# One Mamba block between two feed-forward blocks: GpSimd's running sum of squares moved behind the other work of its pass in one pass of four

## The reference

```python
x = x + 0.5 * ffn(layernorm(x))      # weights by index from a table of 16 values, inner width 688
x = x + mamba2(layernorm(x))
x = x + 0.5 * ffn(layernorm(x))
```

```python
gate, hbc, dt = split(h @ in_proj_w)                # 4096 | 4096 + 2*128 | 64
x, B, C = split(silu(conv4(hbc) + conv_b))          # causal convolution over 4 tokens
y = chunked_scan(x, B, C, softplus(dt + dt_bias), A) + D * x
hidden = y * silu(gate)
var = mean(hidden * hidden, axis=-1)
out = (hidden * rsqrt(var + eps) * norm_w) @ out_proj_w
```

## Time and profile before

| | us |
|---|---|
| median of three executions | 1468.12 (1466.66 to 1471.08) |
| profiled execution, its own time | 1469.74 |
| span of its profile | 1468.0 |
| TensorE busy | 1336.6 |
| VectorE busy | 1190.8 |
| ScalarE busy | 1007.1 |
| GpSimd busy | 823.1 |

### The profile page before, as it was taken

The page is one execution under the profiler, slowest core; times in us unless marked ns, Lnnn a source line. Parts: engine busy times, 40 slices in busy tenths (PEclk is TensorE's granted clock), DMA queues, the critical chain, the costliest instruction groups (busy, mean ns, idle before and its releaser), DMA issues. The chain is left out here.

```text
span 1468.0 us, 27111 instructions
## 1 busy us (share of the span) xinstructions
PE 1336.6 (91%) x8896; PEld 1137.1 (77%) x8896; DVE 1190.8 (81%) x2643; ACT 1007.1 (69%) x2067; POOL 823.1 (56%) x896
## 2 busy tenths in 40 slices
PE   5889887767999999999999999999999999986998
PEld 4778776556888888888888888888888888864887
DVE  5753443576999999999999999999999999986433
ACT  1114433667889988888988898888899888861332
POOL 1004211004678787877878787797787878681000
PEclk9999987978999999999999999999999999995999
DMA  6221000223454554454564645644435544324000
GB/s 128 66 87 36 15 15 0 65 65 76 121 111 98 118 125 114 119 112 98 119 125 115 118 101 114 116 123 121 113 101 109 129 113 117 96 73 186 15 14 29
DMA packets 102085, 136.43 MB, mean 93 GB/s; under 512 B 27744, under 2 KB 49856, under 8 KB 101824
## 3 DMA queue, kind: packets, MB, share of 16 engines
q1 hardware_dynamic: 99840, 132.67, 37.6%
q10 hardware_dynamic: 2112, 2.10, 0.4%
HBM read 124.76 MB, written 9.96 MB: 92 GB/s over the span
## 5 line engine op out<-in xcount | busy, mean ns | idle before, releaser
L845 ACT ACTIVATE M<-cum_row,cum_table 128x128 f32<-128x128 f32 x1024 | 312.2, 390 | 0.0
L1240 DVE SCALAR_TENSOR_TENSOR xs<-psum,conv_w_sb,xs 128x509 f32<-128x509 f32 (+2 forms) x384 | 284.2, 740 | 0.4
L985 POOL TENSOR_TENSOR hid_lo<-hid,hid_hi 128x512 fp32r<-128x512 f32 x128 | 191.2, 1494 | 65.4 <-PE psum L40 59.6
L1028 POOL TENSOR_TENSOR hid<-hid,sg 128x512 f32<-128x512 f32 x128 | 165.7, 1295 | 89.5 <-DVE hid L1308 89.4
L1017 POOL TENSOR_TENSOR squares<-squares,sq 128x512 f32<-128x512 f32 x124 | 160.2, 1292 | 75.2 <-ACT sq L822 75.2
L1267 DVE TENSOR_TENSOR M<-M,CB 128x1024 f32<-128x1024 f32 x128 | 182.9, 1429 | 0.0
L1623 PE MATMUL psum<-M,xdt 128*64 128x128 f32 x2048 | 140.1, 279 | 20.8 <-DVE psum L1299 20.8
L827 ACT ACTIVATE sg<-psum 128x512 f32<-128x512 f32 x128 | 75.2, 587 | 102.2 <-PE psum L40 94.6
L1623 PEld LDWEIGHTS psum<-M,xdt 128*64 128x64 f32 x2048 | 109.9, 136 | 43.2 <-DVE M L1267 25.0
L1600 PE MATMUL psum<-xend,B_tok 128*128 128x128 f32 x1024 | 140.3, 281 | 2.1 <-DVE carry L1291 1.9
L859 ACT ACTIVATE xs<-psum,conv_b_sb,conv_w_sb 128x512 f32<-128x512 f32 x128 | 98.7, 771 | 52.7 <-PE psum L40 52.7
(11 more groups left out here) (210 smaller groups left out, 3432.5 us busy)
## 6 DMA issues: line engine op xcount, KB each, us to landing
cum_row<-cum_scratch SPq DMA_DIRECT2D x256, 256.0 KB, 4.6
e_row<-e_scratch SPq DMA_DIRECT2D x256, 128.0 KB, 3.5
xw_raw<-L_attn_in_proj_w_dram SPq DMA_DIRECT2D x32, 128.0 KB, 5.1
wo_raw<-L_attn_out_proj_w_dram SPq DMA_DIRECT2D x32, 128.0 KB, 4.6
gw_raw<-L_attn_in_proj_w_dram SPq DMA_DIRECT2D x16, 256.0 KB, 5.8
x_res<-_attn_hidden_states_dram ACTq DMA_DIRECT2D x4, 512.0 KB, 9.3
x_scratch<-x_res SPq DMA_DIRECT2D x4, 512.0 KB, 2.6
x_res<-x_scratch SPq DMA_DIRECT2D x1, 2048.0 KB, 7.6
```

The source lines that it names most:

```text
L845: last = nc.scalar.activation(M[:, v % 3, h, c * CH:(c + 1) * CH], cum_row[:, v % 2, h, c * CH:(c + 1) * CH], ACT.Relu, bias=scalar_of(CUM ...
L985: nc.gpsimd.tensor_tensor(hid_lo[:], hid[:, v % 2, :], hid_hi[:, v % 2, :].bitcast(F32), ALU.subtract).then_inc(hid_lo_done, 1)
L1028: nc.gpsimd.tensor_tensor(hid[:, v % 2, :], hid[:, v % 2, :], sg[:, v % 8, :], ALU.mult).then_inc(hid_done, 1)
L1240: nc.vector.scalar_tensor_tensor(xs[:, v % 7, shift:], psum[:, X_BANK + v % 2, 0:TT - shift], tap_of(v, step), xs[:, v % 7, shift:], ALU.m ...
```

## The change

In passes with s % 4 = 1 GpSimd's `add_squares(s)` moves from the head of the pass to behind the gate, the split of hid and, in slot 1, the split of the last output weights. In the code it stands ahead of the other weight splits of the slot table (x weights of slot 5, gate weights of slot 9, output weights of slot 13). In all other passes nothing changes.

```diff
             for s in range(-8, ALL):
-                if alive(s):
+                after_silu = s % GP == 1
+                if alive(s) and not after_silu:
                     add_squares(s)
                 if s == 1:
                     fold_dt(1)
...
                 g, u = divmod(s, SLOTS)
                 if g > 0 and u == 1:
                     split_wo(g * GP + GP - 1)
+                if alive(s) and after_silu:
+                    add_squares(s)
                 if s < 0 or g == GROUPS - 1:
                     continue
                 if u in X_SLOTS:
```

## The result

| | us |
|---|---|
| changed kernel, median of 5 executions | 1480.57 (1480.31 to 1483.36) |
| kernel before, median of 5 executions | 1468.12 (1466.21 to 1471.08) |
| ratio | 1.0086, 95% interval 1.0069 to 1.0103 |
| span of the changed kernel's profile | 1478.6 |

The change makes the kernel 12.4 us slower. The forecast was 1478.6.

A forecast was written before the change was run, and what follows sets the result against it. TensorE was taken to bound the group loop except at named waits. 8.8 us (gate weights) plus 1.7 us (slow clock), all else 0, made 10.5 us on a 1468.1 us median: 1478.6 us, range 1471.5 to 1487 us.

The forecast's parts named there:

- The main term: Slot 9: the moved sum delays the gate weights' low half and so TensorE, 7 x 1.26 = 8.8 us.
- The head of the pass: Where the sum leaves: the gate gains 0.6 us, the low half nothing as it waits for TensorE; worth 0.
- The other signs: Sums wait few us for ScalarE; L1299 scaling wait stays near 17.5 us; no new TensorE waits on ScalarE/VectorE over 5 us.
- The clock term: After the longer gate-weight waits in the loop: one 3.4 us stretch at 1.2 GHz, 1.7 us; bounds 0 to 12.
- Slot 1: Sum behind the output weights makes the square 3.9 us late, VectorE 0.3 us, seven times; taken as 0, bounds 0 to 2.1.
- Rival 2: ScalarE becomes late: later squares in slots 1, 5 and 9 reach TensorE, 4.2 us on top, 1482.8 us; chance 0.12.
- slots 5 and 9: The square starts about 2.5 us later there, hidden in ScalarE's idle time ahead of L827; cost 0.
- rival 4: Faster: the seven gate-weight waits vanish, 5.6 us, and slot 13's gate avoids the product, 3.6 us; 1458.9 us, chance 0.06.
- Beside VectorE: The moved sum runs beside the convolution taps, not the product L1267; cost 0, otherwise 0.73 us in some of 32 passes.
- Rival 3: The sum is hidden: gate weights are ready as before since the low half starts sooner; 1468.1 us, chance 0.09.
- The smaller form of rival 3: Slot 9: 0.34 us gained of each 1.26 us, leaving 6.4 us in all.

The follow-up runs named there:

- experiment 1: Changed kernel, but with the sum of slot 9 back at the head of the pass: 1472.3 us, ratio 1.0025 to the kernel before.
- experiment 2: Kernel before, with the sum moved in slot 9 alone: 1478.8 us, ratio 1.0071.
- experiment 3: Changed kernel, with the sum behind all weight splits of its pass: 1479.4 us, ratio 1.0075 to the kernel before.
- experiment 11: Kernel before, with slot 9's gate weights split first, low halves held behind VectorE's product (s % 4 = 0), slot 9's sum behind the hid split: 1447.7 us.
- experiment 7: Changed kernel, with the low half of the gate weights computed twice in slot 9: 1498.3 us, ratio 1.0201 to the kernel before.
- experiment 5: Kernel before, with the sum moved in slot 1 alone: 1472.2 us, measured once.
- experiment 6: Kernel before, with the sum moved in passes 121 and 125 alone: 1470.3 us, measured once.
- experiment 9: Kernel before, with GpSimd's low half of hid (in slot 0 also the gate) held behind VectorE's product where s % 4 = 0: 1457.8 us, ratio 0.9929.

## Why the prediction was right

*The main term* was right in place, cause and size. It gave 7 x 1.26 = 8.8 us in front of the gate weights; slot 9 measured 8.6, the wait of TensorE 14.2 us where 14.4 were forecast. Experiments 1 and 2 show it from both sides. The head of the pass was worth nothing. In slot 9 that is for the reason given: the low half waits for TensorE. In slot 13 it is not: there the low half starts 1.8 us sooner in the pass, and no slot from 13 to 15 is shorter for it. The sum is harmless to the gate weights once they are split ahead of it, which experiments 3 and 11 show in two ways. The other signs came as listed: sums waited 7.2 us in total for ScalarE, TensorE's wait for the scaling stayed at 17.5 us, and its only new waits on VectorE are 1.7 us in slot 4.

*The clock term*, one slow stretch at 1.7 us, came out as one stretch at 1.6. That it was one and not none or four was luck; experiment 2 had one in seven as well. That such a wait can bring a slow stretch is shown by experiment 7, six of seven, and the cost of one stretch is 1.5 to 1.6 us. Which of seven equal waits is followed by one, no run tells. The full clock of the earlier trace rows begins with the eleventh slice, at 367 us, and not with the ninth; nothing in the sum hangs on it.

*Slot 1* was traced to the right chain and then costed at 0 inside bounds of 0 and 2.1 us. It measured 1.5 us. The step that failed is the one that said "the next named wait of TensorE is a full pass away". VectorE had some lateness left when slot 4 came, two passes on, the slot that had waited for it already. Of the 0.42 us per group about 0.22 arrived. Rival 2 is right in its mechanism, though in the groups only for slot 1 (experiment 5) and at 1.5 and not 4.2 us; for slots 5 and 9 the square's lateness was hidden, as the forecast said.

*The last passes*, 2.8 us, are missing from the forecast. The sum was made for passes that TensorE bounds, 7.6 us long. From pass 120 on there is no projection left and the loop is bound by the chain through GpSimd, so a sum behind the gate delays the square behind it, and that the next gate (experiment 6). It is the late square again, in a place that no rival named.

*Slot 0*, -1.0 us, is the small gain of the change. In slot 13 the gate no longer meets the product, which takes 1.21 us there in place of 1.91, and TensorE's 1.5 us of waits for the recurrence in slot 0 are gone: about 0.14 us per group. It is what rival 4 named, at a quarter of its price. Slot 13 was not moved alone, so this is read from the two traces and not from an experiment.

*Beside VectorE* the sum was rightly costed at 0, but it does disturb VectorE one step on. Behind the moved sum of slot 9 the next gate starts at 804.67, just before the product at 804.84, which takes 2.21 us in place of 1.22. It costs nothing because VectorE waits 1.84 us for TensorE right behind it. *Rival 3*, a hidden sum, and *rival 4*, a faster kernel, did not happen; rival 4's condition (a low half that can start sooner) was the right test, and it failed. The missed terms, +1.5, +2.8 and -1.0, are 3.3 us together in the profiles, and the 12.4 us between the medians lie about 2 us above the forecast's 10.5.

*Two sums of the range* do not come out as written. The main term with none to four slow stretches gives 1476.9 to 1483.7 us, not 1475 to 1484. The smaller form of rival 3 gives 1474.5, so that the range's low end of 1471.5 has no term behind it. Its high end, 1487, lies 4.2 us above rival 2, and no term is named for that either. The measured 1480.6 lies inside the narrower bounds too.

## What to carry to other kernels

When an instruction is moved out of an idle stretch of its queue, look at what stands directly behind its new place and whom that serves; the idle time only changes hands if another engine sets the next start. Idle time in front of a wait is best filled with the work that someone waits for, here the weights, not with work that nobody needs. And a loop's last passes, in which the bounding engine has less to do, need a sum of their own.

## What the runs showed of the hardware

VectorE's product, which reads two SBUF tensors, and GpSimd's instructions hold each other up. Whichever starts first runs at about its own speed, and the other is longer by most of the time that they share. The product starting 0.4 us after a low half took 1.95 us, alone 1.22; the low half starting during a product took 1.92 to 1.94, alone 1.28. Keeping the two apart in the passes with s % 4 = 0, where TensorE had 22 waits behind the product, was worth 14.6 us.

A wait of TensorE of 2.0 us for the gate weights was followed by 3.4 us at 1.2 GHz in two of 14 cases (the changed kernel and experiment 2), one of 3.4 us in six of seven, one of 1.5 us in none of seven (experiment 9), one of up to 0.9 us in none of 22. The 1.94 us wait near the end of the loop, which all 13 kernels have, was followed by such a stretch in seven of the 13 profiles. The price in the middle of the loop was 1.5 to 1.6 us each. The same instructions ahead of the loop took 3.0 us more or less from one profile to another, with the granted clock at 0.92 or 0.94: that is more than any one of the four smaller terms of this case.
